# Fused quantised cross-attention product and low-rank feed-forward on one core: tile 7's second half of normalised x transposed by DMA instead of TensorE

## Chip, core and metric

One core of a Trainium2 chip runs the whole kernel. The metric is the device time of one execution in microseconds (us). Five engines have a part: TensorE (PE in the rows; its weight loads are PEld), VectorE (DVE), ScalarE (ACT), GpSimd (POOL) and SyncE (SP), whose queue issues most of the DMAs. ScalarE issues DMAs too; both queues are served by the core's 16 DMA engines.

## The reference

For x of shape 2 x 1024 x 2048 and a context of shape 2 x 2048 x 2048, with `fake_quant` rounding to 256 levels:

```
x = x + tanh(g_xattn) * (fake_quant(layernorm(x)) @ fake_quant(ctx))
x = x + tanh(g_ffn)   * (layernorm(x) @ (U * S @ V.T).T)
```

V and U are 2048 x 512, so the second step is done as two thin products.

## The kernel before

The 2048 rows of x are 16 tiles of 128 rows; tiles 0 to 7 belong to the first context matrix, tiles 8 to 15 to the second. A tile t goes through these steps:

- `load_x`: four DMAs of 128 x 512 into a ring of four tiles (`ring`); each waits until the tile four before has been stored. `quantise` and `op2` on ScalarE round the normalised tile to fp16 (`qn`), `q_transpose` (a DMA transpose on SyncE's queue) turns it over into `qT`.
- `s1`: the first product, tile by quantised context (`q2`), in four column units of 16 matmuls. VectorE (`x1_unit`) adds each unit to x.
- second layernorm; ScalarE (`x_hi_half`) and VectorE (`x_lo_half`) write the result as a high and a low fp16 part into `xs`, in two halves g = 0 and 1 of 1024 columns each. Each half is then transposed into `xT[:, g]`.
- `mm3`: V product of the transposed halves, 24 matmuls for g = 0 and then 24 for g = 1. ScalarE (`hid_hi`) and VectorE (`hid_lo`) write the result as two fp16 parts, `h_transpose` (a DMA transpose) turns them over.
- `mm4`: U product, four units of 12 matmuls in three PSUM banks in turn. VectorE (`y_unit`) adds each to x, `store` writes it out. Unit i may start once `y_unit` i-3 is done.

Two normalised halves are transposed by a DMA each (`x_transpose_half`, 128 x 2048 fp16, 512 KB) for all tiles but one: tile 7 (`X_PE`). For it TensorE does the transposes (`x_pieces(g)`, 16 pieces of 128 x 128 for each half, into two PSUM banks), and VectorE copies the two banks to `xT` (`xT_copy(g)`).

All engines run an order written out by hand. Around tile 7 TensorE's is `mm3(6)`, `x_pieces(0)`, `mm4(5)`, `x_pieces(1)`, `mm3(7)`, `mm4(6)`, `colsum_of_sums(0)` to `(2)`, `mm4(7, 0, 3)` and then `s1_part(8, 0)`. In the same stretch the second context matrix is brought in: 32 chunks of 512 KB, loaded by DMAs that ScalarE issues (`refill`) right after the chunk that it has read (`op1`, line 925: to uint8, read from `stage`, `corr`, `qn` or `q2` itself), turned into fp16 by GpSimd (line 293), and summed by VectorE (`k_sum`) for the column corrections. ScalarE's own order there is chunks 17 to 21, `hid_hi(6)`, chunks 22 to 25, `sums1(8)`, chunks 26 to 29, `quantise(8)`, `op2(8)`, chunks 30 and 31, `hid_hi(7)`. SyncE's queue is in order, and it waits at the head: four stores of tile 4, four loads of tile 8, `h_transpose(6)`, then `turn(5, False)`, which is stores of tile 5 in turn with loads of tile 9, then `q_transpose(8)`, `h_transpose(7)`.

Of the kernel before, what the change touches and what calls it, by code (L numbers as in the profile page):

```python
# [7 lines left out]
def gated_block_program(nc, x, ctx_in, params, U_t, S, V, out):  # L8
    f32, bf16, f16 = mybir.dt.float32, mybir.dt.bfloat16, mybir.dt.float16
# [3 lines left out]
    P = 128  # L13
# [7 lines left out]
    TB = SEQ // P  # L21
# [8 lines left out]
    X_PE = TB - 1  # L30
# [14 lines left out]
    with es:  # L45
# [14 lines left out]
        xs = sb("xs", [P, 2, 2, HW], f16)  # L60
        xT = sb("xT", [P, 2, 2, KT // 2, P], f16)
# [145 lines left out]
        unit_bank = lambda t, n: bank[4 * (n % 2) + t] if t < G else bank[(s_unit(t, n) - NQ * G) % 3]  # L207
        colsum_bank = lambda b, n: bank[4 * (n % 2) + 3] if b == 0 else bank[(0, 1, 3, 4)[n]]
        h_bank = lambda u: bank[3 + u % 2]
        x_dma = lambda u: u + 1 - (u > X_PE)  # L210
        x_bank = lambda g, half: bank[(2 * g + half) % 3]
        y_bank = lambda i: bank[5 + i % 3]
        k_sums = lambda n: xn[:, 0:W].bitcast(f16) if n == 0 else xs[:, n // 3, (n - 1) % 2, :]
        chunk = lambda c: (c // CB, c % CB // CQ, c % CQ)
# [129 lines left out]
        def _(sp):  # L344
            def load_x(t, n):
                if t >= R:
                    sp.wait_ge(y_stored[t % R][n], 16 * (t // R))
                sp.dma_start(xq(t, n), x_rows[t * P:(t + 1) * P, n * W:(n + 1) * W]).then_inc(x_in[t % R][n], 16)
# [51 lines left out]
            def h_transpose(u):  # L400
                sp.wait_ge(h_hi, u + 1)
                sp.wait_ge(h_lo, u + 1)
                if u == 0:
                    sp.wait_ge(sq_done, 16)
                if u == NT - 1:
                    sp.wait_ge(p_done, 2 * NP * len(PAIRS))
                elif u == TB - 1:
                    sp.wait_ge(ctx_u8, act_u8(STAGE1_CHUNK))
                elif u == 5:
                    sp.wait_ge(s1_done, S1_END(6))  # L410
                elif u >= 1:
                    sp.wait_ge(y_done, NQ * {6: 5, 8: 7}.get(u, u))
                sp.dma_start_transpose(hT_of(u), hs.rearrange("p k w -> p (k w)")).then_inc(hT_in, 16)
# [175 lines left out]
        def _(pe):  # L589
# [27 lines left out]
            def colsum_of_sums(n):  # L617
                pe.wait_ge(k_summed, KS * (n + 1))
                if n < 2:
                    pe.wait_ge(xT_copied, 4)  # L620
                else:
                    pe.wait_ge(h_hi, TB - 1 + n - 2)
                    pe.wait_ge(h_lo, TB - 1 + n - 2)
                for a in range(CK):
                    mm = nc.tensor.matmul(colsum_bank(1, n)[:, :], ones_h[:, :], k_sums(n)[:, a * W:(a + 1) * W],
                                          start=(a == 0), stop=(a == CK - 1))
                mm.then_inc(colsum_done, 1)
# [113 lines left out]
            def mm3(u):  # L741
                if u == 0:
                    pe.wait_ge(corr_ready, NQ - 1)
                elif u == 1:
                    pe.wait_ge(x1_ready, unit(0, NQ - 1) + 1)
                    pe.wait_ge(norm_ready, 1)
                else:
                    pe.wait_ge(h_hi, u - 1)
                    pe.wait_ge(h_lo, u - 1)
                if u == TB:  # L750
                    pe.wait_ge(corr_ready, 2 * NQ)
                for g in range(2):
                    if u == X_PE:
                        pe.wait_ge(xT_copied, 2 * g + 2)
                    else:
                        pe.wait_ge(xT_in[g], 16 * x_dma(u))
                    for a, k in enumerate(KORD[g]):
                        if u == 0 and a % 2 == 0:
                            pe.wait_ge(split_hi, VORD.index(k // 2) + 1)
                        for half in range(2):  # L760
                            nc.tensor.matmul(h_bank(u)[:, :], x_home(u, g)[:, half, k % 8, :], v_hl[:, k, 0, :],  # L761
                                             start=(g == 0 and a == 0 and half == 0), stop=False)
                    for a, k in enumerate(KORD[g]):
                        if u == 0 and a % 2 == 0:
                            pe.wait_ge(split_lo, VORD.index(k // 2) + 1)
                        mm = nc.tensor.matmul(h_bank(u)[:, :], x_home(u, g)[:, 0, k % 8, :], v_hl[:, k, 1, :],  # L766
                                              start=False, stop=(g == 1 and a == 7))
                    mm.then_inc(mm3_half, 1)

            def x_pieces(g):  # L770
                pe.wait_ge(xs_hi, 2 * X_PE + g + 1)
                pe.wait_ge(xs_lo, 2 * X_PE + g + 1)
                for half in range(2):
                    if 2 * g + half < 3:
                        pe.wait_ge(x1_ready, S1_END(TB - 1) - (2, 1, 0)[2 * g + half])
                    else:
                        pe.wait_ge(xT_copied, 1)
                    dst = x_bank(g, half)[:, :].bitcast(f16)
                    for k in range(8):
                        mm = nc.tensor.transpose(dst[:, k * P:(k + 1) * P], xs[:, g, half, k * P:(k + 1) * P], ident[:, :])  # L780
                    mm.then_inc(xT_written, 1)

            def mm4(u, n0=0, n1=NQ):
# [133 lines left out]
        def _(act):  # L917
# [85 lines left out]
            def x_hi_half(u, g):  # L1003
                scale, bias = ln2[:, u % 2, 8:9], ln2[:, u % 2, 9:10]
                act.wait_ge(ln2_ready, u + 1)
                if u in first_of and g == 0:
                    act.wait_ge(p_done, 2 * NP * (first_of[u] + 1))
                if u - 1 == X_PE:
                    act.wait_ge(xT_written, 2 * g + 2)
                elif u > 0:  # L1010
                    act.wait_ge(xT_in[g], 16 * x_dma(u - 1))
                nc.scalar.activation(xs[:, g, 0, :], xhalf(u, g), ACT.Identity, bias=bias, scale=scale).then_inc(xs_hi, 1)  # L1012
                if u in XN_ACT:
                    act.wait_ge(xs_lo, 2 * u + g)
                    nc.scalar.activation(xn[:, :], xhalf(u, g), ACT.Identity, bias=bias, scale=scale).then_inc(xn_ready, 1)  # L1015
# [226 lines left out]
        def _(dve):  # L1242
# [125 lines left out]

            def early_t1():
                for g in range(2):  # L1370
                    dve.wait_ge(xT_in[g], 16 * x_dma(EARLY[0] - 1))
                for c in range(2):
                    b11, b12 = [k_piece(flat2(b_part(n, 0)), c, 2 * HW) for n in (2, 3)]
                    tt(k_piece(e_t1, c, 2 * HW), b12, b11, ALU.subtract).then_inc(e_t1_made, 1)
# [64 lines left out]
            def t4(q, c0, c1):  # L1439
                p, j = divmod(q, 2)  # L1440
                for c in range(c0, c1):
                    if c == 0:
                        dve.wait_ge(t_made, 4 * j + 4)
                        if j == 0:
                            for g in range(2):
                                dve.wait_ge(xT_in[g], 16 * x_dma(PAIRS[p][0] - 1))
                        else:
                            dve.wait_ge(p_done, pdone(q - 1, P4))
                    tt(k_piece(t4_room, c, HW), k_piece(flat2(b_part(2 * j, 1)), c, HW),
                       k_piece(t2_room[j], c, HW), ALU.subtract).then_inc(t4_made, 1)  # L1450
# [67 lines left out]
                x_lo_half(u, 0)  # L1518
                x_lo_half(u, 1)

            def xT_copy(g):
                for half in range(2):
                    dve.wait_ge(xT_written, 2 * g + half + 1)
                    dve.wait_ge(mm3_half, 2 * (X_PE - 1) + g + 1)
                    nc.vector.tensor_copy(xT[:, g, half, :, :].rearrange("p k w -> p (k w)"),
                                          x_bank(g, half)[:, :].bitcast(f16)).then_inc(xT_copied, 1)
# [7 lines left out]
            def k_sum(n, i):  # L1534
                c = CB + CQ * n + i
                dve.wait_ge(q2_pool, pool_count(c))
                if i == 1 and n == 0:
                    dve.wait_ge(xs_lo, 2 * TB)
                elif i == 1:
                    dve.wait_ge(xT_written, 2 + 2 * (n // 3))  # L1540
                else:
                    dve.wait_ge(k_summed, KS * n + i - 1)
                tt(k_sums(n), q2_chunk(c - 1) if i == 1 else k_sums(n), q2_chunk(c), ALU.add).then_inc(k_summed, 1)
# [358 lines left out]
```

## Time and profile before

| | us |
|---|---|
| median of 3 runs | 586.42 |
| lowest, highest | 584.85, 586.98 |
| profiled execution, device time | 585.22 |
| its span in the trace | 583.4 |
| TensorE busy in it | 566.6 (97%) |

Times in the rows are us from the start of the span, and "[... <-X]" is idle time of the engine just before and what ended it. Matmuls are pipelined: the times from one matmul's start to the next one's tell what it costs, not its length. `x3` in a row is a run of three instructions. For a DMA, the length of a queue row (SPq, ACTq) is the time of issuing; the time to landing is told by other rows.

### The profile page before, as it was taken

The numbers are of one execution on the slowest core, as the hardware profiler recorded it, in microseconds if no ns is written. First come the engines' busy times: TensorE is split into PE (matmuls) and PEld (weight loads), VectorE is DVE, ScalarE is ACT, GpSimd is POOL, SyncE is SP. The second block draws the span as 40 slices with busy tenths as digits, with TensorE's granted clock in tenths as the row PEclk, the third lists the DMA queues.
The fourth block names the chain that finished last, engine by engine and source line by source line (L and its number), as shares of the span: only waits on it lengthen the run. The fifth ranks groups of instructions, "written<-read, shape, count | busy, mean of one in ns | idle before, by whom it ended". The sixth has DMA issues, their size and how long they took to land.

```text
span 583.4 us, 7494 instructions
## 1 busy us (share of the span) xinstructions
PE 566.6 (97%) x2672; PEld 258.1 (44%) x2672; DVE 450.0 (77%) x795; ACT 251.7 (43%) x282; POOL 195.8 (34%) x146
## 2 busy tenths in 40 slices
PE   1999999999999999999999999999999999999997
PEld 0444444444444444444444444444444444444444
DVE  6878889997978851788879798788598986889222
ACT  5899978823214525537883612103530135003200
POOL 2999750000750038836543720210044005310000
PEclk9999999999999999999999999999999999999999
DMA  8999995639558986799986362424854086403612
GB/s 277 387 387 386 345 265 135 127 107 188 138 157 170 256 175 164 278 222 386 272 202 174 61 137 52 126 73 80 216 102 143 2 184 159 126 1 74 161 55 108
DMA packets 146997, 103.00 MB, mean 177 GB/s; under 512 B 109840, under 2 KB 110096, under 8 KB 146960
## 3 DMA queue, kind: packets, MB, share of 16 engines
q1 hardware_dynamic: 137968, 85.22, 55.5%
q10 hardware_dynamic: 8992, 17.30, 9.3%
q8 instruction: 21, 0.34, 0.2%
q14 instruction: 16, 0.13, 0.1%
HBM read 58.99 MB, written 16.78 MB: 130 GB/s over the span
## 4 chain that ended last, share of the span: by engine, by line
PE 82%; DVE 5%; DMA 5%; ACT 4%; issue 2%; SPq 1%; POOL 1%; ACTq 1%; DVEq 0%
PE bank L761 17%; PE bank L653 15%; PE bank L698 12%; PE bank L811 8%; PE bank L812 8%; PE bank L766 8%; PE bank L816 8%; DMA stage<-in_ctx_dram 3%; PE bank L612 2%; PE bank L728 2%; ACT u8r L925 2%; DMA ring<-in_x_dram 1%; DVE qn L1314 1%; POOL q L293 1%; DVE xn L1512 1%
## 5 line engine op out<-in xcount | busy, mean ns | idle before, releaser
L299 POOL TENSOR_SCALAR ring<-ring,bvec 128x2048 f32<-128x2048 f32 x16 | 34.5, 2155 | 256.6 <-DVE bvec L1326 256.6
L653 PE MATMUL bank<-q,qT 128*128 128x512 f16 x448 | 104.3, 383 | 0.7 <-DMA qT<-qn 0.7
L761 PE MATMUL bank<-v_hl,xT 128*128 128x512 f16 x448 | 101.3, 379 | 0.0
L304 POOL TENSOR_TENSOR ring<-ring,corr 128x512 f32<-128x512 f32 x64 | 87.6, 1399 | 19.1 <-ACT corr L1040 18.1
L293 POOL TENSOR_SCALAR q<-u8r,const 128x1024 f16<-128x1024 uint8 x52 | 67.0, 1298 | 36.8 <-ACT u8r L925 33.4
L811 PE MATMUL bank<-u_hl,hbuf 128*128 128x512 f16 x208 | 78.9, 379 | 0.1
L812 PE MATMUL bank<-u_hl,hbuf 128*128 128x512 f16 x208 | 78.9, 379 | 0.0
L996 ACT ACTIVATE ln<-ln,const 128x1 f32<-128x1 f32 x16 | 4.7, 293 | 151.7 <-DVE ln L1485 151.2
L653 PEld LDWEIGHTS bank<-q,qT 128*128 128x128 f16 x448 | 44.0, 98 | 54.8 <-issue 1.4
L761 PEld LDWEIGHTS bank<-v_hl,xT 128*128 128x128 f16 x448 | 43.8, 98 | 52.4 <-DMA xT<-xs 0.2
L1559 DVE SCALAR_TENSOR_TENSOR ring<-bank,cy,ring 128x512 f32<-128x512 f32 x63 | 45.9, 743 | 13.5 <-PE bank L816 13.4
L816 PE MATMUL bank<-u_hl,hbuf 128*128 128x512 f16 x208 | 53.4, 379 | 0.0
L766 PE MATMUL bank<-v_hl,xT 128*128 128x512 f16 x224 | 52.9, 379 | 0.0
L1515 DVE TENSOR_TENSOR xs<-xn,xs 128x1024 f16<-128x1024 f32 x32 | 42.9, 1340 | 12.7 <-ACT xn L1015 6.4
L1012 ACT ACTIVATE xs<-ring,ln 128x1024 f16<-128x1024 f32 x32 | 38.6, 1234 | 16.8 <-DVE ln L1497 10.6
L1283 DVE BATCH_NORM_STATS2 st<-ring 128x6 f32<-128x512 f32 x56 | 35.2, 679 | 8.4 <-DMA ring<-in_x_dram 8.3
L1475 DVE SCALAR_TENSOR_TENSOR ring<-bank,const,ring 128x512 f32<-128x512 f32 x42 | 31.3, 746 | 9.8 <-PE bank L698 9.8
L1531 DVE SCALAR_TENSOR_TENSOR hbuf<-bank,hbuf 128x512 f16<-128x512 f32 x16 | 11.0, 687 | 33.5 <-ACT hbuf L1027 33.4
L766 PEld LDWEIGHTS bank<-v_hl,xT 128*128 128x128 f16 x224 | 21.9, 98 | 26.5
L925 ACT ACTIVATE u8r<-stage,par,const 128x1024 uint8<-128x1024 f32 x22 | 27.2, 1236 | 13.9 <-DMA stage<-in_ctx_dram 9.8
L1344 DVE SCALAR_TENSOR_TENSOR ring<-bank,const,ring 128x512 f32<-128x512 f32 x36 | 26.7, 741 | 8.4 <-PE bank L653 5.0
L612 PE MATMUL bank<-q,ones_h 128*128 128x512 f16 x64 | 20.4, 402 | 11.9 <-POOL q L293 11.9
(200 smaller groups left out, 832.7 us busy)
## 6 DMA issues: line engine op xcount, KB each, us to landing
out_dram<-ring SPq DMA_DIRECT2D x63, 256.0 KB, 3.5
ring<-in_x_dram SPq DMA_DIRECT2D x62, 256.0 KB, 4.3
v_hl<-in_ctx_dram SPq DMA_DIRECT2D x26, 512.0 KB, 11.5
stage<-in_ctx_dram ACTq DMA_DIRECT2D x17, 512.0 KB, 6.0
u_hl<-in_L_ffn_V_dram SPq DMA_DIRECT2D x8, 512.0 KB, 11.5
corr<-in_ctx_dram ACTq DMA_DIRECT2D x8, 512.0 KB, 6.8
stage<-in_ctx_dram SPq DMA_DIRECT2D x6, 512.0 KB, 11.4
q<-in_ctx_dram ACTq DMA_DIRECT2D x4, 512.0 KB, 10.7
```

The lines of the kernel that those rows point to most:

```text
L293: nc.gpsimd.tensor_scalar(q2_chunk(c), u8r[:, c % NU8, :], C_NC2, 1.0, ALU.add, ALU.mult)\
L304: nc.gpsimd.tensor_tensor(xq(t, n), xq(t, n), corr[:, n * W:(n + 1) * W], ALU.add).then_inc(x1_pre, 1)
L653: mm = nc.tensor.matmul(unit_bank(t, n)[:, :], qT_of(t)[:, k, :], q2[:, n, k, :], start=(k == 0), stop=(k == KT - 1))
L698: mm = nc.tensor.matmul(pbank(q, k)[:, :], left[:, i, :], right[:, i, :], start=(i == 0 and k in (P1, P2, P5)), stop=(i == KH - 1), skip_g ...
L761: nc.tensor.matmul(h_bank(u)[:, :], x_home(u, g)[:, half, k % 8, :], v_hl[:, k, 0, :], start=(g == 0 and a == 0 and half == 0), stop=False)
L766: mm = nc.tensor.matmul(h_bank(u)[:, :], x_home(u, g)[:, 0, k % 8, :], v_hl[:, k, 1, :], start=False, stop=(g == 1 and a == 7))
L811: nc.tensor.matmul(y_bank(i)[:, :], t_hi[:, r, :], u_hl[:, n, r, 0, :], start=(r == 0), stop=False)
L812: nc.tensor.matmul(y_bank(i)[:, :], t_lo[:, r, :], u_hl[:, n, r, 0, :], start=False, stop=False)
L816: mm = nc.tensor.matmul(y_bank(i)[:, :], t_hi[:, r, :], u_hl[:, n, r, 1, :], start=False, stop=(r == RT - 1))
L925: nc.scalar.activation(u8r[:, c % NU8, :], flat2(SPOT[c][0]), ACT.Identity, bias=P_Z2, scale=C_R2).then_inc(ctx_u8, 1)
L1515: tt(xs[:, g, 1, :], xn[:, :], xs[:, g, 0, :], ALU.subtract).then_inc(xs_lo, 1)
L1559: stt(xq(u, n), y_bank(i)[:, :], cy[:, n:n + 1], xq(u, n), ALU.mult, ALU.add).then_inc(y_ready, 1)
```

## The change

Tile 7's half g = 0 stays on TensorE and VectorE. Half g = 1 is transposed by a DMA on SyncE's queue, put between the loads of tile 8 and `h_transpose(6)`. `x_pieces(1)` leaves TensorE's order and `xT_copy(1)` VectorE's. The second half of `mm3(7)`, the later users of `xs` half 1 (`x_hi_half(8, 1)`, `k_sum` of the fourth column group) wait for the DMA's semaphore `xT_in[1]` instead. The DMA waits for the high and low parts of tile 7's half 1 and for the end of `mm3(6)`, which reads the same half of `xT`.

```
                 load_x(8, n)
+            x_transpose_half(7, 1)
             h_transpose(6)
...
-                    if u == X_PE:
-                        pe.wait_ge(xT_copied, 2 * g + 2)
+                    if u == X_PE and g == 0:
+                        pe.wait_ge(xT_copied, 2)
                     else:
-                        pe.wait_ge(xT_in[g], 16 * x_dma(u))
+                        pe.wait_ge(xT_in[g], 16 * x_dma(u, g))
...
-            x_pieces(0)
+            x_pieces()
             mm4(5)
-            x_pieces(1)
             mm3(7)
...
-                if u - 1 == X_PE:
-                    act.wait_ge(xT_written, 2 * g + 2)
+                if u - 1 == X_PE and g == 0:
+                    act.wait_ge(xT_written, 2)
...
+                elif i == 1 and n < 3:
+                    dve.wait_ge(xT_written, 2)
                 elif i == 1:
-                    dve.wait_ge(xT_written, 2 + 2 * (n // 3))
+                    dve.wait_ge(xT_in[1], 16 * x_dma(X_PE, 1))
...
-            xT_copy(0)
+            xT_copy()
...
             y_unit(5, 3)
-            xT_copy(1)
             quantise(8)
```

TensorE from the end of `mm4(5)` to the end of `mm3(7)`, before (L780 is `x_pieces`, L761 and L766 are `mm3`):

```order
L816 MATMUL bank<-u_hl,qT 128x512 x4
L780 MATMUL bank<-ident,xs 128x128 [waits x1_ready,xs_lo,xs_hi]
L780 MATMUL bank<-ident,xs 128x128 x7
L780 MATMUL bank<-ident,xs 128x128 [waits xT_copied]
L780 MATMUL bank<-ident,xs 128x128 x7
L761 MATMUL bank<-v_hl,xT 128x512 [waits xT_copied,h_lo,h_hi]
L761 MATMUL bank<-v_hl,xT 128x512 x15
L766 MATMUL bank<-v_hl,xT 128x512 x8
L761 MATMUL bank<-v_hl,xT 128x512 [waits xT_copied]
L761 MATMUL bank<-v_hl,xT 128x512 x15
L766 MATMUL bank<-v_hl,xT 128x512 x8
```

and after (the same lines are L814, L762 and L767 there):

```order
L814 MATMUL bank<-u_hl,qT 128x512 x4
L762 MATMUL bank<-v_hl,xT 128x512 [waits xT_copied,h_lo,h_hi]
L762 MATMUL bank<-v_hl,xT 128x512 x15
L767 MATMUL bank<-v_hl,xT 128x512 x8
L762 MATMUL bank<-v_hl,xT 128x512 [waits xT_in1]
L762 MATMUL bank<-v_hl,xT 128x512 x15
L767 MATMUL bank<-v_hl,xT 128x512 x8
```

The 16 pieces are gone, and the second half of `mm3(7)` waits for the DMA's semaphore.

SyncE's queue at the same place, before and after in one (L424 are stores, L348 loads of x, L413 `h_transpose`, L393 `x_transpose_half`):

```order
 L424 DMA out_dram<-ring 128x512 x4
 L348 DMA ring<-in_x_dram 128x512 x4
+L393 DMA_TRANSPOSE xT<-xs 128x16x128
 L413 DMA_TRANSPOSE hbuf<-hbuf 128x8x128
 L424 DMA out_dram<-ring 128x512 x2
```

One DMA is added, and `h_transpose(6)` and all that follows stand behind it.

## Rows read from the trace of the kernel before

**Rows 1.** Page: busy time by engine.

```profile
PE 566.6 (97%) x2672; PEld 258.1 (44%) x2672; DVE 450.0 (77%) x795; ACT 251.7 (43%) x282; POOL 195.8 (34%) x146
```

**Rows 2.** TensorE's timeline, 267 to 303 us: start, length, line, tiles, count.

```profile
267.09 1.89 PE L766 MATMUL bank<-v_hl,xT 128*128 128x512 f16 x8
...
280.07 1.06 PE L780 MATMUL bank<-ident,xs 128*128 128x128 f16 x16
280.96 3.62 PE L761 MATMUL bank<-v_hl,xT 128*128 128x512 f16 x16
...
286.14 3.62 PE L761 MATMUL bank<-v_hl,xT 128*128 128x512 f16 x16
...
291.32 0.38 PE L811 MATMUL bank<-u_hl,hbuf 128*128 128x512 f16 x1
...
299.10 0.38 PE L811 MATMUL bank<-u_hl,hbuf 128*128 128x512 f16 x1
...
302.98 0.38 PE L811 MATMUL bank<-u_hl,stage 128*128 128x512 f16 x1
```

**Rows 3.** VectorE's timeline, 280 to 299 us.

```profile
280.98 1.27 DVE L1525 COPY xT<-bank 128x1024 f16<-128x1024 f16 x2
284.01 0.15 DVE L1299 TENSOR_SCALAR ln<-ln 128x1 f32<-128x1 f32 x1 [1.76 <-ACT ln L987]
...
297.36 1.40 DVE L1559 SCALAR_TENSOR_TENSOR ring<-bank,cy,ring 128x512 f32<-128x512 f32 x2
```

**Rows 4.** VectorE and TensorE's weight loads at 255 us: `y_unit(4, 0)`, `mm4(4, 3)`.

```profile
255.06 0.74 DVE L1559 SCALAR_TENSOR_TENSOR ring<-bank,cy,ring 128x512 f32<-128x512 f32 x1
...
255.85 0.10 PEld L811 LDWEIGHTS bank<-u_hl,hbuf 128*128 128x128 f16 x1 [0.64 <-DVE ring L1559]
```

**Rows 5.** ScalarE's timeline, 277 to 297 us.

```profile
277.11 1.24 ACT L925 ACTIVATE u8r<-corr,par,const 128x1024 uint8<-128x1024 f32 x1
...
287.37 1.24 ACT L925 ACTIVATE u8r<-stage,par,const 128x1024 uint8<-128x1024 f32 x1 [0.51 <-ACT u8r L925]
...
294.89 1.23 ACT L925 ACTIVATE u8r<-stage,par,const 128x1024 uint8<-128x1024 f32 x1
296.02 0.57 ACT L1027 ACTIVATE hbuf<-bank 128x512 f16<-128x512 f32 x1
```

**Rows 6.** SyncE's queue, 246 to 275 us: start, time of issuing.

```profile
246.07 8.46 SPq L393 DMA_TRANSPOSE xT<-xs  x2
...
260.50 7.92 SPq L348 DMA_DIRECT2D ring<-in_x_dram  x4
274.05 1.23 SPq L413 DMA_TRANSPOSE hbuf<-hbuf  x1
```

**Rows 7.** Issued at 246.03, 247.78 and 246.07, 265.17, 270.42, 286.89: us to landing.

```profile
corr<-in_ctx_dram ACTq DMA_DIRECT2D x1, 512.0 KB, 4.2
...
corr<-in_ctx_dram ACTq DMA_DIRECT2D x1, 512.0 KB, 7.0
xT<-xs SPq DMA_TRANSPOSE x1, 8.9
...
corr<-in_ctx_dram ACTq DMA_DIRECT2D x1, 512.0 KB, 11.9
...
stage<-in_ctx_dram ACTq DMA_DIRECT2D x1, 512.0 KB, 11.1
...
stage<-in_ctx_dram ACTq DMA_DIRECT2D x1, 512.0 KB, 7.1
```

**Rows 8.** Transposes issued at 274.05 and 297.38 us: us to landing.

```profile
hbuf<-hbuf SPq DMA_TRANSPOSE x1, 7.9
...
stage<-hbuf SPq DMA_TRANSPOSE x1, 3.1
```

**Rows 9.** Stretches: us; busy PE, PEld, DVE, ACT, POOL; clock, DMA share, GB/s.

```profile
273.00:278.00 5.00, 5.00 (x25) 2.29 (x24) 4.79 (x7) 4.01 (x4) 4.42 (x4) 1.00 1.05 388
...
282.00:288.00 6.00, 6.00 (x29) 2.73 (x28) 3.92 (x10) 4.95 (x6) 2.66 (x2) 1.00 0.75 237
```

More of the change, by code:

```diff
@@ L209, in gated_block_program @@
         h_bank = lambda u: bank[3 + u % 2]
-        x_dma = lambda u: u + 1 - (u > X_PE)
-        x_bank = lambda g, half: bank[(2 * g + half) % 3]
+        x_dma = lambda u, g: u + 1 - (g == 0 and u > X_PE)
+        x_bank = lambda half: bank[half]
         y_bank = lambda i: bank[5 + i % 3]
@@ L619, in colsum_of_sums @@
                 if n < 2:
-                    pe.wait_ge(xT_copied, 4)
+                    pe.wait_ge(xT_copied, 2)
                 else:
@@ L752, in mm3 @@
                 for g in range(2):
-                    if u == X_PE:
-                        pe.wait_ge(xT_copied, 2 * g + 2)
+                    if u == X_PE and g == 0:
+                        pe.wait_ge(xT_copied, 2)
                     else:
-                        pe.wait_ge(xT_in[g], 16 * x_dma(u))
+                        pe.wait_ge(xT_in[g], 16 * x_dma(u, g))
                     for a, k in enumerate(KORD[g]):
@@ L768, in mm3, with x_pieces @@
                     mm.then_inc(mm3_half, 1)
-            def x_pieces(g):
-                pe.wait_ge(xs_hi, 2 * X_PE + g + 1)
-                pe.wait_ge(xs_lo, 2 * X_PE + g + 1)
+            def x_pieces():
+                pe.wait_ge(xs_hi, 2 * X_PE + 1)
+                pe.wait_ge(xs_lo, 2 * X_PE + 1)
                 for half in range(2):
[L774 to L778, printed above, removed]
+                    pe.wait_ge(x1_ready, S1_END(TB - 1) - (2, 1)[half])
+                    dst = x_bank(half)[:, :].bitcast(f16)
                     for k in range(8):
-                        mm = nc.tensor.transpose(dst[:, k * P:(k + 1) * P], xs[:, g, half, k * P:(k + 1) * P], ident[:, :])
+                        mm = nc.tensor.transpose(dst[:, k * P:(k + 1) * P], xs[:, 0, half, k * P:(k + 1) * P], ident[:, :])
                     mm.then_inc(xT_written, 1)
@@ L1007, in x_hi_half @@
                     act.wait_ge(p_done, 2 * NP * (first_of[u] + 1))
-                if u - 1 == X_PE:
-                    act.wait_ge(xT_written, 2 * g + 2)
+                if u - 1 == X_PE and g == 0:
+                    act.wait_ge(xT_written, 2)
                 elif u > 0:
-                    act.wait_ge(xT_in[g], 16 * x_dma(u - 1))
+                    act.wait_ge(xT_in[g], 16 * x_dma(u - 1, g))
                 nc.scalar.activation(xs[:, g, 0, :], xhalf(u, g), ACT.Identity, bias=bias, scale=scale).then_inc(xs_hi, 1)
@@ L1370, in early_t1 @@
                 for g in range(2):
-                    dve.wait_ge(xT_in[g], 16 * x_dma(EARLY[0] - 1))
+                    dve.wait_ge(xT_in[g], 16 * x_dma(EARLY[0] - 1, g))
                 for c in range(2):
@@ L1445, in t4 @@
                             for g in range(2):
-                                dve.wait_ge(xT_in[g], 16 * x_dma(PAIRS[p][0] - 1))
+                                dve.wait_ge(xT_in[g], 16 * x_dma(PAIRS[p][0] - 1, g))
                         else:
@@ L1519, in x_lo, with xT_copy @@
                 x_lo_half(u, 1)
-            def xT_copy(g):
+            def xT_copy():
                 for half in range(2):
[L1523 to L1526, printed above, removed]
+                    dve.wait_ge(xT_written, half + 1)
+                    dve.wait_ge(mm3_half, 2 * (X_PE - 1) + 1)
+                    nc.vector.tensor_copy(xT[:, 0, half, :, :].rearrange("p k w -> p (k w)"),
+                                          x_bank(half)[:, :].bitcast(f16)).then_inc(xT_copied, 1)
             def hid_lo(u):
```

## Prediction

> **What bounds the kernel now.** I read first the page: TensorE is busy for 97% of the span [rows 1], so a change counts only by what it takes off TensorE's row of work or by the idle time that it puts into it. Second, TensorE's timeline around tile 7: from 280 to 303 us each matmul follows the one ahead without a bracket, so nothing waits there now [rows 2]. Third, the timelines of VectorE and ScalarE, read backwards from the matmuls that they release, for the distance that each release has to the matmul behind it: that is the room in which the other engines may get late, and it shrinks by whatever TensorE gains. Fourth, the DMAs one by one, from issue to landing, since the change puts 512 KB of transpose into a stretch in which the DMA engines have no free time: 388 GB/s at a share of 1.05 [rows 9].
>
> **The pieces.** TensorE starts the 16 pieces at 280.07 and the first matmul of mm3(7) at 280.96 [rows 2]. Without them mm3(7) starts at 280.07: 0.89 us less, all of it on the path. Nothing else leaves TensorE.
>
> **The two copies.** They take 1.27 us of VectorE, and right behind them VectorE idles 1.76 us for ScalarE's root [rows 3]. Without them it idles 1.27 us longer. Cost and gain 0; the cover is ScalarE's row of chunks, which ends at the same time as before.
>
> **The wait in mm3(7).** The DMA can't be issued before mm3(6) has ended, at 267.09 + 1.89 = 268.98 [rows 2]; SyncE's queue has issued tile 8's last load by 260.50 + 7.92 = 268.42 [rows 6], so it goes out at about 269.0. The second half of mm3(7) wants it at 286.14 - 0.89 = 285.25 [rows 2]. Early bound of its landing: the half issued at 246.07 took 8.9 us [rows 7], which gives 277.9. Late bound: it is served when the whole backlog is through, which is when the context chunk issued at 270.42 lands, 281.5, plus its own share of the DMA engines. That share I take from two chunks: 4.2 us for the one issued just ahead of the transpose of 246.07, and 7.0 us for the one issued behind it, so 2.8 us [rows 7]. That gives 284.3. Both bounds lie ahead of 285.25: the wait costs 0. Queued behind it on TensorE is everything, so if it were late, each us would be one of the total.
>
> **The queue behind the new DMA.** h_transpose(6) goes out at 274.05 when VectorE has made its input [rows 6]. Two transposes of this size took 8.46 us to issue, 4.2 each [rows 6]: SyncE would be free at 273.2, just ahead. Landing was 7.9 us later, at 282.0 [rows 8]; with 2.8 us more, 284.8, against a need at 291.32 - 0.89 = 290.43 [rows 2]. Cost 0. The stores of tile 5, the loads of tile 9, q_transpose(8) and h_transpose(7) stand behind it too; the last of these is a rival below.
>
> **The loads beside it.** Here the sum is decided. In the same 10 us ScalarE reads context chunks as they land: the one issued at 265.17 took 11.9 us, landed at 277.07 and was read from 277.11 on [rows 5, 7]. ScalarE then has work without a gap worth naming through to hid_hi(7) at 296.02 [rows 5], hid_lo(7) on VectorE waits for that, and the y_unit right behind it, (6, 0), starts at 297.36 [rows 3]. So if this chunk lands d us later, hid_hi(7) and y_unit(6, 0) come d us later. mm4(6, 3) needs y_unit(6, 0) (unit i behind y_unit i-3). One such unit lasts 0.74 us and its matmul can load 0.05 us behind its end [rows 4]: it is released at 297.36 + 0.74 + 0.05 = 298.15, and starts now at 299.10 [rows 2]. With the gain it would start at 298.21. The room is 0.95 us now and 0.06 us then: **the gain of 0.89 us fits just in, and every us of d beyond 0.06 is a us of TensorE idle**. The change in time is the larger of -0.89 and d - 0.95.
>
> What is d? The trace of before has no transpose in such a backlog except one, and I bound it from both sides. *Low end, 0:* h_transpose(6) was issued at 274.05 with four chunks ahead of it and took 7.9 us, where the same transpose in a calmer place (297.38) took 3.1 [rows 8]; the chunk issued just ahead of the transpose of 246.07 landed in 4.2 us, unharmed, while the one behind it took 7.0 [rows 7]. Both say that a transpose takes its turn behind the chunks issued ahead of it, and that only those issued behind it pay. The chunk of 265.17 was issued 3.8 us ahead of the new DMA: d = 0. *High end, 4.2:* the new transpose is served at once and takes its 2.8 us, and h_transpose(6), half as large, comes right behind it and takes 1.4 more before the chunk has landed. The nearest row in time, load and kind is that of 274.05, so I take d = 0. The chunk that pays then is that of 270.42: it landed at 281.5 and is read at 287.37 [rows 5, 7], 5.8 us of room for 2.8.
>
> The page "DMA: Bandwidth & Descriptors" of the Trainium skill, section "Queues, rings and completion order", speaks against this choice: each DMA engine goes round between the queues that have work, a packet at a time, so a transpose on SyncE's queue would start beside ScalarE's chunks and not behind them. By that rule the chunk of 265.17 is late and the first rival holds; by the row of 274.05 it isn't.
>
> **Sum.** 585.22 (profiled execution) - 0.89 + 0 + 0 + 0 = 584.3 us. The median of the runs stands 1.2 us above that execution, so the forecast for the median is 586.42 - 0.89 = 585.5 us. VectorE and ScalarE follow TensorE in the later tiles, so I expect the 0.89 us to reach the end.
>
> **Rivals.**
> 1. *The transpose shares the DMA engines with the chunks (slower).* d = 2.8: mm4(6, 3) waits, 2.8 - 0.95 = +1.85, 588.3 us; with h_transpose(6) in front of the chunk as well, d = 4.2, +3.25, 589.7 us. It decides from d = 0.95 on. For it: the 7.0 us of the chunk behind a transpose, and DMA engines with no free time. Against it: the 7.9 and the 4.2 us. The skill's rule above is this case.
> 2. *The same 2.8 us turn up later.* The chunk issued at 286.89 took 7.1 us, landed at 293.99 and was read at 294.89 [rows 5, 7]: 0.90 us of room. If the added work is still in the queues then, d = 2.8 - 0.9 = 1.9 and the change is +0.95, 587.4 us. Against it: from 282 to 288 us the DMA engines moved 237 GB/s only [rows 9], so there is room to catch up.
> 3. *SyncE's queue is held.* If issuing stalls until the backlog is through, all behind it goes out late, h_transpose(7) too. It landed at 297.38 + 3.1 = 300.5 [rows 8], and is wanted at 302.98 - 0.89 = 302.1 [rows 2]: 1.6 us of room. Late by 2.5 us, it would eat the gain: 586.4 us.
> 4. *The change doesn't do what it says:* the wait on the DMA takes the place of the pieces. At the worst it starts when the backlog is through, 281.5, and then takes the 7.0 us of a DMA in mixed traffic [rows 7]: 288.5, 3.2 us of idle time in mm3(7), +2.3, 588.8 us.
>
> **How the numbers follow.** Forecast (no new wait above 0.3 us) 0.50; rival 1 0.25, of which 0.06 at its high end; rival 2 0.10; rival 3 0.10; rival 4 0.05. About 0.5% is what a measurement of this kernel can tell from no change, 2.9 us: below 583.5 or above 589.3. Even the whole gain is a third of that, so faster has only the scatter of the runs, 0.02; slower is the high end of rival 1 and some scatter, 0.08; same 0.90. The range runs from 584.7 (the forecast less 0.8 of scatter; the three runs spread over 2.1) to 588.5 (rival 1's first price): outside are the high end of rival 1 and tails.
>
> **What would show each step.** Right: mm3(7) starts 0.89 us earlier with no bracket, its second half too; the chunk of 265.17 is still read at 277.1 and hid_hi(7) starts at 296.0; the new transpose takes over 9 us to land, and the chunk of 270.42 lands near 284. Wrong by rival 1: ScalarE waits for a DMA at 277 us, hid_hi(7) starts at 298 or later, and the weight load of mm4(6, 3) has a bracket ending in VectorE's y_unit. By rival 2 that bracket with the wait at 294; by rival 3 a bracket at mm4(7, 0) that ends in a DMA; by rival 4 one in the middle of mm3(7). What would make the forecast wrong beyond these: a place behind 310 us where TensorE has under 0.89 us of room, which gives the gain back unseen.

## Result

| | us |
|---|---|
| kernel before, median of 14 runs | 585.22 (584.58 to 587.51) |
| changed kernel, median of 14 runs | 586.31 (585.04 to 588.27) |
| ratio, changed to before | 1.0020, 95% interval 1.0011 to 1.0029 |

The change costs 1.1 us, 0.2%. That lies within the stated range, but on the other side of zero from the forecast of -0.9. The changed kernel's runs fall into groups: five of them lie from 585.0 to 585.4 and six from 587.0 to 588.3, where the kernel before has two (587.0 and 587.5). An execution at a lower granted clock is left out of the ratios below (one each in e9 and e10).

### The profile after

Its span is 583.4 us, as before, but it had reached the stretch in question 0.45 us earlier for reasons that lie ahead of the change. So times are compared from a common mark, the start of the first 16 pieces: 268.82 us before, 268.37 after. TensorE's timeline after (start, length, line, tiles; L778 are the pieces, L762 mm3, L809 the first matmul of a unit of mm4), which answers to [rows 2]:

```profile
268.37 1.06 PE L778 MATMUL bank<-ident,xs 128*128 128x128 f16 x16
...
279.63 3.62 PE L762 MATMUL bank<-v_hl,xT 128*128 128x512 f16 x16
...
284.81 3.62 PE L762 MATMUL bank<-v_hl,xT 128*128 128x512 f16 x16
...
299.02 0.39 PE L809 MATMUL bank<-u_hl,hbuf 128*128 128x512 f16 x1 [1.10 <-DVE ring L1558]
...
302.91 0.38 PE L809 MATMUL bank<-u_hl,stage 128*128 128x512 f16 x1
...
341.33 3.62 PE L762 MATMUL bank<-v_hl,xT 128*128 128x512 f16 x16
```

From the mark to mm3(7) it is 11.26 us, and was 12.14: the gain of the pieces is there (0.88 us), and the second half of mm3(7) starts without a bracket. Then mm4(6, 3) waits for VectorE. At mm3(8), 341.33, TensorE is 72.96 us from the mark, and was 341.40 - 268.82 = 72.58: a loss of 0.38 us in this execution, -0.89 + 1.27.

VectorE and ScalarE after, which answer to [rows 3] and [rows 5] (L1558 is y_unit, L922 reads a context chunk, L1024 is hid_hi):

```profile
298.22 1.40 DVE L1558 SCALAR_TENSOR_TENSOR ring<-bank,cy,ring 128x512 f32<-128x512 f32 x2
```

```profile
275.89 1.24 ACT L922 ACTIVATE u8r<-q,par,const 128x1024 uint8<-128x1024 f32 x1 [1.36 <-DMA q<-in_ctx_dram]
277.42 1.24 ACT L922 ACTIVATE u8r<-corr,par,const 128x1024 uint8<-128x1024 f32 x1 [0.28 <-DMA corr<-in_ctx_dram]
...
289.36 1.24 ACT L922 ACTIVATE u8r<-corr,par,const 128x1024 uint8<-128x1024 f32 x1 [0.44 <-DMA corr<-in_ctx_dram]
...
296.88 0.57 ACT L1024 ACTIVATE hbuf<-bank 128x512 f16<-128x512 f32 x1
```

hid_hi(7) stands 28.51 us behind the mark, and stood 27.20: d = 1.31. The first 0.76 of it is there at the chunk read at 277.42. The rest comes with the chunk read at 289.36, for which ScalarE waits now and didn't before.

SyncE's queue after, which answers to [rows 6]:

```profile
268.62 8.30 SPq L393 DMA_TRANSPOSE xT<-xs  x1
277.04 3.71 SPq L413 DMA_TRANSPOSE hbuf<-hbuf  x1
...
296.42 3.00 SPq L375 DMA_TRANSPOSE qT<-qn  x1
299.53 1.24 SPq L413 DMA_TRANSPOSE stage<-hbuf  x1
```

The new transpose needs 8.3 us to be issued. h_transpose(6) goes out 3 us later than before. Behind it stand the stores of tile 5, which take 9.3 us to land where the first two took 6.4 and 5.6, and the loads of tile 9, which wait for these stores; so q_transpose(8) and h_transpose(7) are late too, the latter by 2.2 us. The landings, issued at 264.83, 268.62, 277.04 and 278.69, each row by itself from a list of DMAs:

```profile
corr<-in_ctx_dram ACTq DMA_DIRECT2D x1, 512.0 KB, 12.6
...
xT<-xs SPq DMA_TRANSPOSE x1, 15.5
...
hbuf<-hbuf SPq DMA_TRANSPOSE x1, 12.5
...
corr<-in_ctx_dram ACTq DMA_DIRECT2D x1, 512.0 KB, 10.6
```

The transpose lands at 284.1, against a need at 284.8; h_transpose(6) at 289.5, against 290.0. The last row is the chunk that is read at 289.36; the same chunk took 5.8 us in the kernel before. And the stretches, against [rows 9] (us; busy PE, PEld, DVE, ACT, POOL; clock, DMA share, GB/s):

```profile
273.00:278.00 5.00, 5.00 (x25) 2.28 (x24) 4.79 (x7) 3.36 (x4) 3.95 (x3) 1.00 1.06 294
...
282.00:288.00 6.00, 6.00 (x29) 2.74 (x28) 3.36 (x9) 4.95 (x6) 2.35 (x2) 1.00 1.18 166
```

From 273 to 278 us the DMA engines move 294 GB/s where they moved 388. Finer stretches show where that comes from:

```profile
273.50:274.50 1.00, 1.00 (x7) 0.44 (x5) 0.90 (x3) 1.00 (x1) 1.00 (x1) 1.00 0.36 20
...
275.00:278.00 3.00, 3.00 (x16) 1.37 (x14) 2.90 (x4) 1.82 (x2) 2.44 (x3) 1.00 1.09 390
```

For about 1.2 us they move next to nothing (20 GB/s), and then the old rate again with the transpose's packets among the chunks'. Such a stall stands in all eight traces with a transposing DMA at this place of the queue (after, e2, e3, e5, e6, e8, e9, e10; 25 GB/s from 274 to 275 in e2, 11 from 273.75 to 274.75 in e9), and from 273 to 278 us in none of the five others (e4, with a plain DMA there, has 393 GB/s). What stalls them isn't known.

From 282 to 288 us they move only 166 GB/s at a share of 1.18, where before there were 237 at 0.75. From 282 to 286 a packet of ScalarE's queue takes 0.28 us, and took 0.09 (116 packets in 50.6% of 16 engines' time, and 259 in 36.5%). This is when the chunk issued at 278.69 is under way.

### The profile page after: what moved, and what is told of

Read it like the earlier page. It is cut to its first block, busy times and chain, and to the rows that moved or that the text cites. A ratio compares the mean times of both kernels' runs of the same rounds, so it can differ in the third digit from the quotient of the medians.

```text
span 583.4 us, 7459 instructions
## 1 busy us (share of the span) xinstructions
PE 565.9 (97%) x2656; PEld 257.7 (44%) x2656; DVE 448.5 (77%) x793; ACT 252.0 (43%) x282; POOL 194.7 (33%) x146
## 4 chain that ended last, share of the span: by engine, by line
PE 74%; DMA 9%; ACT 6%; DVE 5%; issue 3%; SPq 1%; ACTq 1%; POOL 1%; DVEq 0%
PE bank L654 15%; PE bank L762 14%; PE bank L699 12%; PE bank L809 7%; PE bank L814 7%; PE bank L767 7%; PE bank L810 7%; DMA corr<-in_ctx_dram 4%; DMA stage<-in_ctx_dram 3%; ACT u8r L922 3%; PE bank L613 2%; PE bank L729 2%; DMA ring<-in_x_dram 2%; ACTq L929 1%; DVE qn L1311 1%
## 5 line engine op out<-in xcount | busy, mean ns | idle before, releaser
L762 PE MATMUL bank<-v_hl,xT 128*128 128x512 f16 x448 | 101.3, 379 | 0.0
L809 PE MATMUL bank<-u_hl,hbuf 128*128 128x512 f16 x208 | 78.9, 379 | 1.2 <-DVE ring L1558 1.1
L293 POOL TENSOR_SCALAR q<-u8r,const 128x1024 f16<-128x1024 uint8 x52 | 65.5, 1267 | 39.2 <-ACT u8r L922 36.3
L762 PEld LDWEIGHTS bank<-v_hl,xT 128*128 128x128 f16 x448 | 43.9, 98 | 52.6
L1558 DVE SCALAR_TENSOR_TENSOR ring<-bank,cy,ring 128x512 f32<-128x512 f32 x63 | 45.9, 744 | 13.3 <-PE bank L814 13.2
L814 PE MATMUL bank<-u_hl,hbuf 128*128 128x512 f16 x208 | 53.4, 379 | 0.0
L767 PE MATMUL bank<-v_hl,xT 128*128 128x512 f16 x224 | 52.9, 379 | 0.0
L1009 ACT ACTIVATE xs<-ring,ln 128x1024 f16<-128x1024 f32 x32 | 38.6, 1234 | 16.5 <-DVE ln L1494 10.6
L1472 DVE SCALAR_TENSOR_TENSOR ring<-bank,const,ring 128x512 f32<-128x512 f32 x42 | 31.3, 746 | 9.8 <-PE bank L699 9.8
L767 PEld LDWEIGHTS bank<-v_hl,xT 128*128 128x128 f16 x224 | 21.9, 98 | 26.4
L922 ACT ACTIVATE u8r<-stage,par,const 128x1024 uint8<-128x1024 f32 x22 | 27.2, 1236 | 13.4 <-DMA stage<-in_ctx_dram 9.8
L809 PEld LDWEIGHTS bank<-u_hl,hbuf 128*128 128x128 f16 x208 | 20.4, 98 | 27.5 <-DVE ring L1558 3.6
```

Of the source, the lines that this page charges most:

```text
L293: nc.gpsimd.tensor_scalar(q2_chunk(c), u8r[:, c % NU8, :], C_NC2, 1.0, ALU.add, ALU.mult)\
L809: nc.tensor.matmul(y_bank(i)[:, :], t_hi[:, r, :], u_hl[:, n, r, 0, :], start=(r == 0), stop=False)
L814: mm = nc.tensor.matmul(y_bank(i)[:, :], t_hi[:, r, :], u_hl[:, n, r, 1, :], start=False, stop=(r == RT - 1))
L922: nc.scalar.activation(u8r[:, c % NU8, :], flat2(SPOT[c][0]), ACT.Identity, bias=P_Z2, scale=C_R2).then_inc(ctx_u8, 1)
L1558: stt(xq(u, n), y_bank(i)[:, :], cy[:, n:n + 1], xq(u, n), ALU.mult, ALU.add).then_inc(y_ready, 1)
```

## Experiments

The theory after the result had two parts. **A**: the transpose makes ScalarE's chunks late, so that y_unit(6, 0) is late for mm4(6, 3). **C**: it holds SyncE's queue, so that h_transpose(6) and (7) come late for mm4(6) and mm4(7). The rivals: **B**, mm3(7) waits for the new DMA itself in the slower executions; and that the pieces never give anything back. **D** and **E** ask whether the form of the DMA or its bytes do the harm.

In all tables "in the trace" is the way from the mark (the first pieces) to the start of mm3(8), less the 72.58 us of the kernel before. It is one execution; the ratio is from the timed runs, against the kernel before on the same chip.

### e1: the gain alone

```
-            x_transpose_half(7, 1)
```

(and `x_dma` counts one DMA less for half 1)

> As the changed kernel, but the new DMA isn't issued: the second half of mm3(7) reads what xT held for tile 6, so that half of tile 7's transpose is left out. It prices the pieces alone. Both theories: mm3(7) starts 0.89 us earlier and nothing waits behind it: -0.9 us against the kernel before. If it comes out at 0 or above, the loss of the changed kernel isn't from the DMA at all, and there is a place behind 310 us that gives the gain back.

Measured: ratio 0.9986 (0.9974 to 0.9997), -0.8 us; in the trace 71.68, -0.90. The first matmul of mm4(7) is where it should be, with no bracket since the mark:

```profile
269.16 1.06 PE L777 MATMUL bank<-ident,xs 128*128 128x128 f16 x16
...
302.43 0.38 PE L808 MATMUL bank<-u_hl,stage 128*128 128x512 f16 x1
```

The price of the pieces and its way to the end were right. The whole loss against this kernel, about 1.9 us, comes from the DMA.

### e2: the DMA alone

```
+            sp.dma_start_transpose(qT[:, 0, :, :], flat2(xs[:, 1, :, :])).then_inc(extra_in, 16)
             h_transpose(6)
```

(into the kernel before, with its pieces; later writers of `qT` half 0 and of `xs` half 1 wait for `extra_in`)

> The kernel before with all its pieces and copies, plus one more DMA transpose of the same 512 KB at the same place of SyncE's queue, into a free buffer (half of qT) that no matmul reads. It prices the DMA alone. Theory A (the transpose makes ScalarE's context chunks late, hid_hi(7) and y_unit(6, 0) come late, mm4(6, 3) waits): the same end as the changed kernel, +0.4 to +1.1 us, with a bracket at mm4(6, 3). Theory B (mm3(7) waits for the new DMA in the slower executions, which landed 0.5 us ahead of its need in the profile): nothing reads it here, so at most +0.4.

Measured: ratio 1.0007 (0.9997 to 1.0017), +0.4 us; in the trace 72.78, +0.20. The chunk lateness is there (hid_hi(7) 27.96 us from the mark, d = 0.76), inside the room of 0.95, and mm4(6, 3) doesn't wait. The weight load of mm4(7) does, and for the other reason:

```profile
269.19 8.19 SPq L536 DMA_TRANSPOSE qT<-xs  x1
```

```profile
303.28 0.10 PEld L818 LDWEIGHTS bank<-u_hl,stage 128*128 128x128 f16 x1 [0.52 <-DMA stage<-hbuf]
```

So in this trace the DMA costs something where no one reads its result (the interval of the runs reaches below 1), and it does so by SyncE's queue. From the mark h_transpose(6) goes out 3.3 us later and the first stores of tile 5 4.6 us later; these take 8.9 us to land where they took 6.4, and h_transpose(7) is 2.7 us late behind the loads that wait for them. The hold of 8.2 us and the slower stores aren't separated here. The expectation's bracket at mm4(6, 3) was missed, and the two theories' numbers met at +0.4, so this run doesn't rule out B; the two traces of the changed kernel don't show it (e5).

### e3: y_unit(6, 0) ahead of hid_lo(7)

```
+            y_unit(6, 0)
             hid_lo(7)
             row_correction(8)
-            y_unit(6, 0)
```

> The changed kernel with one move on VectorE: y_unit(6, 0) ahead of hid_lo(7), so that mm4(6, 3) no longer stands behind ScalarE's chunks. Theory A: the wait of 1.1 us at mm4(6, 3) goes, the next need is mm4(7, 0) with some 0.4 us of room, so -0.9 to -0.3 us against the kernel before. Theory B (late landing in mm3(7)) or C (SyncE's queue held, h_transpose(7) late): it stays at +0.5 to +1.1.

Measured: ratio 1.0003 (0.9990 to 1.0016), +0.2 us; in the trace 73.64, +1.06. The wait at mm4(6, 3) is gone as meant, and others have its place:

```profile
302.93 0.60 PE L626 MATMUL bank<-xs,ones_h 128*128 128x512 f16 x2 [0.64 <-DVE xs L1542]
304.38 0.39 PE L809 MATMUL bank<-u_hl,stage 128*128 128x512 f16 x1 [0.84 <-DMA stage<-hbuf]
```

The first is the column sums, whose sum on VectorE (L1542) stands behind hid_lo(7); the second is h_transpose(7), issued at 300.40 behind q_transpose(8) at 297.22. A third is smaller: the weight load of mm4(6, 0) waits 0.45 us for h_transpose(6). Both parts, A and C, are at work here, so the removal of one wait uncovers others. The forecast of A alone, -0.9 to -0.3, was missed.

### e4: a plain DMA of the same bytes

```
-            x_transpose_half(7, 1)
+            sp.dma_start(xT[:, 1, :, :, :]..., xs[:, 1, :, :]...).then_inc(xT_in[1], 16)
```

(with the same waits ahead of it)

> The changed kernel with a plain DMA of the same 512 KB from xs to xT in place of the transposing one: tile 7's second half isn't transposed. Theory D (it is the form, a transpose of very many small packets that hangs behind the chunks and holds SyncE's queue 8 us): the plain DMA issues in under 1 us, lands within 8 us, the chunks are late by at most 1 us; 0 to -0.9 us. Theory E (it is the bytes, any 512 KB in a full stretch): d of 1 to 1.5 us as in the changed kernel, +0.3 to +1.1.

Measured: ratio 0.9994 (0.9982 to 1.0005), -0.35 us; in the trace 72.46, -0.12.

```profile
269.22 0.55 SPq L534 DMA_DIRECT2D xT<-xs  x1
```

```profile
xT<-xs SPq DMA_DIRECT2D x1, 512.0 KB, 8.0
```

```profile
277.84 1.24 ACT L925 ACTIVATE u8r<-corr,par,const 128x1024 uint8<-128x1024 f32 x1 [0.69 <-DMA corr<-in_ctx_dram]
...
298.89 0.39 PE L812 MATMUL bank<-u_hl,hbuf 128*128 128x512 f16 x1 [0.37 <-DVE ring L1561]
```

The weight load of mm4(7, 0) waits too, 0.54 us, for h_transpose(7), which takes 4.8 us to land here (3.1 before).

Neither D nor E alone. The bytes make the first chunks late in either form (0.58 us from the mark at the chunk of 277.84, against 0.76). The transposing form adds the hold of the queue, 8.3 us against 0.55, and the landing of 15.5 against 8.0.

### e5: the changed kernel once more

> The changed kernel itself, on the chip of the runs beside it, for a second trace. Theory A (ScalarE's chunks late) and theory C (SyncE's queue held for 8 us, so that h_transpose(6), tile 9's loads, q_transpose(8) and h_transpose(7) come late) both say +0.5 to +1.2 us; A has its bracket at mm4(6, 3), C has one at mm4(6, 0) or mm4(7, 0) that ends in a DMA.

Measured: ratio 1.0013 (1.0001 to 1.0026), +0.8 us. The trace is of the slowest of the 12 executions (588.92), 74.31 from the mark, +1.73:

```profile
293.35 0.39 PE L809 MATMUL bank<-u_hl,hbuf 128*128 128x512 f16 x1 [0.80 <-DMA hbuf<-hbuf]
...
302.67 0.39 PE L809 MATMUL bank<-u_hl,hbuf 128*128 128x512 f16 x1 [1.38 <-DVE ring L1558]
```

```profile
293.00 1.24 ACT L922 ACTIVATE u8r<-corr,par,const 128x1024 uint8<-128x1024 f32 x1 [1.30 <-DMA corr<-in_ctx_dram]
```

```profile
hbuf<-hbuf SPq DMA_TRANSPOSE x1, 13.1
```

Both brackets that A and C named stand in one trace: mm4(6, 0) waits for h_transpose(6), issued at 280.17 and 13.1 us on its way, and mm4(6, 3) for y_unit(6, 0) behind a chunk that ScalarE waited 1.3 us for. Without the first wait the second would be longer by as much: y_unit(6, 0) stands behind ScalarE's chain until 301.87, long after its unit of mm4(6) is ready. So h_transpose(6) costs nothing by itself here. mm3(7) has no bracket, so B isn't seen in either trace of the changed kernel; nor in e3 and e8, where the same DMA lands 1.3 and 1.6 us ahead of its need. It landed 0.7 and 0.6 us ahead in the two of the changed kernel.

### e6: a shorter queue of chunks

```
-                act.dma_start(SPOT[c][0], ctx_k[...])
+                part = slice(0, 1) if SPOT[c][1] in room_in else slice(0, CK)
+                act.dma_start(SPOT[c][0][:, part, :], ctx_k[...][:, part, :])
```

> The changed kernel with the four context chunks that go to q2 itself loaded by half (256 KB each; the other half of those chunks is left out), so that the queue of ScalarE's loads is 1 MB shorter when the new transpose is issued. If the loss is contention (theories A and C alike), SyncE's queue is held well under 8 us, the transpose lands before 282, no wait is left and the gain shows: -0.9 to -0.4 us. If the hold of SyncE's queue comes from the transpose itself, whatever else is in flight, it stays at +0.5 to +1.1.

Measured: ratio 0.9983 (0.9975 to 0.9992), -1.0 us; in the trace 71.69, -0.89: the whole gain.

```profile
268.53 6.79 SPq L393 DMA_TRANSPOSE xT<-xs  x1
```

```profile
xT<-xs SPq DMA_TRANSPOSE x1, 11.0
```

The hold is still 6.8 us, more than expected ("well under 8"), and does no harm: the transpose lands at 279.5, ScalarE's chunks have no bracket, and h_transpose(7) is issued at 295.96. With 1 MB less in the queue the change does what it is for: the loss needs the full queue. The stall of the DMA engines is in this trace too (77 GB/s from 273.5 to 274.25), but ScalarE's chunks land ahead of their reads, so nothing waits for it. This run shortens the chunks' own way too, so it doesn't part A from C.

### e7: the new DMA behind h_transpose(6)

```
-            x_transpose_half(7, 1)
             h_transpose(6)
+            x_transpose_half(7, 1)
```

> The changed kernel with the new DMA behind h_transpose(6) on SyncE's queue instead of ahead of it. Theory A: the chunk that was issued at 265.17 isn't touched, d falls to about 0 there; the transpose is issued at 275 and lands at about 285, so mm3(7)'s second half waits 0 to 1.5 us: -0.9 to +0.6. Theory C: the hold of the queue only begins 6 us later and ends later, tile 9's loads and h_transpose(7) come as late as before or later: +0.5 to +2.

Measured: ratio 1.0093 (1.0080 to 1.0107), +5.4 us; in the trace +5.74. Further out than either expectation:

```profile
290.14 5.31 PE L762 MATMUL bank<-v_hl,xT 128*128 128x512 f16 x16 [4.78 <-DMA xT<-xs]
```

```profile
xT<-xs SPq DMA_TRANSPOSE x1, 14.3
```

The DMA is issued at 275.81 and takes 14.3 us again, so mm3(7) waits 4.8 us. The 16 matmuls behind the wait take 5.31 us where they took 3.62: TensorE's granted clock was 1.00 through the wait and until 290.5, 0.50 (the lower of its levels of 1.2 and 2.4 GHz) from 291 to 294, and 1.00 again from 294.5. That is 1.7 us of the 5.7. Theory A was right in its first half: the chunk read at 277 us isn't late (ScalarE is back at its place before, sums1(8) 10.27 us from the mark against 10.47). But the transpose then makes the chunk issued at 278.13 late, as in the changed kernel: it takes 11.8 us, and ScalarE waits 1.55 us for it.

### e8: h_transpose(7) ahead of q_transpose(8)

```
-            q_transpose(8)
             h_transpose(7)
+            q_transpose(8)
```

(on top of e3)

> The changed kernel with y_unit(6, 0) ahead of hid_lo(7) on VectorE (as the third experiment) and, on SyncE's queue, h_transpose(7) ahead of q_transpose(8). If what was left in the third experiment is h_transpose(7) behind a late q_transpose(8) (theory C), mm4(7, 0) has over 1 us of room again: -0.7 us against the kernel before, with a wait of about 0.4 us left at mm4(6, 0) in some executions. If theory A alone were true, this does no more than the third one: +0.2.

Measured: ratio 1.0031 (1.0020 to 1.0041), +1.8 us; in the trace +1.42. The wait at mm4(7, 0) is gone, as expected, but the gain isn't there:

```profile
303.82 1.91 ACT L978 ACTIVATE qn<-ring 128x2048 uint8<-128x2048 f32 x1 [7.42 <-DMA qT<-qn]
```

```profile
310.67 7.07 PE L654 MATMUL bank<-q,qT 128*128 128x512 f16 x32 [1.03 <-ACT corr L1037]
```

h_transpose(7) has to wait for hid_lo(7), so q_transpose(8) behind it goes out at 298.53. ScalarE's sums1(9) waits for q_transpose(8), the column corrections come behind it, and s1(8) waits for those. sums1(9) starts 5.0 us later from the mark than in the kernel before, and s1(8) 1.2 us later than the gain of the pieces would have it: this third chain had 3.8 us of room, and the swap of two transposes used up more than that.

### e9 and e10: half the DMA

```
-            x_transpose_half(7, 1)
+            sp.dma_start_transpose(xT[:, 1, 0, :, :], xs[:, 1, 0, :]).then_inc(xT_in[1], 16)
             h_transpose(6)
...
             mm4(5)
+            x_low_piece()
...
             y_unit(5, 3)
+            xT_low_copy()
```

(waits left out; 8 pieces and one copy come back for the low parts; e10 has e3's move too)

> The changed kernel with the DMA cut to half its size: only the high parts of tile 7's second half go by DMA (256 KB, same place of the queue), the low parts by 8 pieces on TensorE and one copy on VectorE as before. Theory C (a transpose of 512 KB behind a full queue holds SyncE 8 us because its packets don't fit; one of 256 KB was issued in 1.2 us at the same place): no hold, h_transpose(6) issued by 274.1, no wait at mm4(6, 0) or mm4(7, 0). The pieces give 0.45 us, the chunk is late by about half of 0.7 us, inside the room: -0.45 us. If the hold is there all the same: 0 to +0.8.

> The same as e9 with y_unit(6, 0) ahead of hid_lo(7) on VectorE: -0.45 us too if nothing waits in e9, and a little under e9 if mm4(6, 3) still waits there.

Measured: e9 0.9994 (0.9985 to 1.0004), in the trace 72.13, -0.45; e10 0.9986 (0.9977 to 0.9995), in the trace 72.15, -0.43. Neither has a bracket on the matmuls from the mark to s1(8).

```profile
268.55 1.24 SPq L533 DMA_TRANSPOSE xT<-xs  x1
272.96 3.97 SPq L413 DMA_TRANSPOSE hbuf<-hbuf  x1
```

```profile
xT<-xs SPq DMA_TRANSPOSE x1, 12.8
```

Issued in 1.24 us, so SyncE reaches h_transpose(6) in time; that one takes 3.97 us to issue in turn, but SyncE is free at 276.9, and not at 280.8 as in the changed kernel. The landing is still 12.8 us (13.5 in e10), against 15.5 for twice the size. In the medians e9 stands at -0.6 and e10 at -0.8 us. ScalarE's lateness differs between the two traces: hid_hi(7) is 27.40 us from the mark in e9 and 28.19 in e10, d = 0.20 and 0.99. With the gain of 0.45 the room at mm4(6, 3) is 0.95 - 0.45 = 0.50, so by an estimate e9's order would have cost some 0.5 us in an execution like that of e10's trace, and there e3's move is what saves it.

### e11: the control

```
+            y_unit(6, 0)
             hid_lo(7)
```

(the same move as e3, in the kernel before)

> The kernel before with that one move on VectorE alone: mm4(6, 3) had 0.95 us of room already, so 0. It is the control for the third experiment: if it gains by itself, part of what the third one gained over the changed kernel isn't about the DMA.

Measured: ratio 0.9993 (0.9984 to 1.0002), and 0.00 in the trace. It can't be told from no change; nor can it from the -0.4 us that its median shows, so how much of e10's 0.8 us is the move's alone stays open. **e10 is below both kernels with its interval**, by 0.14% of the kernel before; its trace shows 0.43 us of that.

### All of them

| | ratio (95%) | in the trace, us | bracket on TensorE, (w) on a weight load alone |
|---|---|---|---|
| changed | 1.0020 (1.0011 to 1.0029) | +0.38 | mm4(6, 3) |
| e1 no DMA | 0.9986 (0.9974 to 0.9997) | -0.90 | none |
| e2 DMA added to before | 1.0007 (0.9997 to 1.0017) | +0.20 | mm4(7, 0) (w) |
| e3 y_unit first | 1.0003 (0.9990 to 1.0016) | +1.06 | mm4(6, 0) (w), column sums, mm4(7, 0) |
| e4 plain DMA | 0.9994 (0.9982 to 1.0005) | -0.12 | mm4(6, 3), mm4(7, 0) (w) |
| e5 changed again | 1.0013 (1.0001 to 1.0026) | +1.73 | mm4(6, 0), mm4(6, 3), mm4(7, 0) (w) |
| e6 1 MB less in flight | 0.9983 (0.9975 to 0.9992) | -0.89 | none |
| e7 behind h_transpose(6) | 1.0093 (1.0080 to 1.0107) | +5.74 | mm3(7) |
| e8 h_transpose(7) first | 1.0031 (1.0020 to 1.0041) | +1.42 | s1(8), column sums |
| e9 half the DMA | 0.9994 (0.9985 to 1.0004) | -0.45 | none |
| e10 half, y_unit first | 0.9986 (0.9977 to 0.9995) | -0.43 | column sums (w) |
| e11 y_unit first in before | 0.9993 (0.9984 to 1.0002) | 0.00 | none |

## The prediction, step by step

**The pieces: right.** 0.89 us forecast, 0.88 in the trace, 0.8 in e1's runs, and it reaches the end.

**The copies: right.** VectorE idles 3.46 us where it idled 1.76: 1.27 for the copies, and the rest since ScalarE's root comes later. Nothing waits for it.

**The wait in mm3(7): right, with some luck.** The late bound, 284.3 for 285.25, is nearly what happened (284.1 for 284.8). It is so since two errors nearly cancel: counted from the mark, the last chunk of the backlog landed 0.9 us later than in the kernel before, and the transpose 2.2 us behind it and not 2.8. Nor did the transpose wait for its turn behind the backlog; its packets ran among the chunks'. Of the 0.95 us of room that the bound leaves, 0.68 was there.

**The queue behind: wrong.** I took 4.2 us to issue from the pair at 246.07, which met a much shorter queue of chunks. It was 8.3, and h_transpose(6) landed at 289.5 where I had 284.8. I had the mechanism as rival 3 at 0.10, priced it by h_transpose(7) alone, and didn't see h_transpose(6). In the changed kernel's second trace mm4(6, 0) waits 0.8 us for it, inside the longer wait of the chunks. Of the three DMAs that TensorE waits for, h_transpose(7) had the least room in the first trace: it lands at 302.64 for 302.91, h_transpose(6) at 289.50 for 289.99, and the new one at 284.13 for 284.81.

**The loads beside: the step that decided, and it failed.** The relation was right: with d = 1.31, d - 0.95 gives +0.36, and the trace has +0.38. In the second trace hid_hi(7) is 29.77 us from the mark, d = 2.57, which gives +1.62 for +1.73. What failed is the size, d = 0. The choice of the low end was half right: the chunk issued ahead of the transpose was late by 0.76 us only, not by 2.8. But I checked the room of the chunk issued just behind the transpose (270.42) and passed over the next one, issued at 278.4. The prediction doesn't name it. By then the transpose and the held h_transpose(6) were the backlog. It took 10.6 us where it had taken 5.8, and used up its 4.3 us of room and 0.44 more. That is rival 2's mechanism, with a chunk 8 us earlier than the one that I named, and rival 1 at a quarter of its price on top.

The row that I took d = 0 from was misread as well. At 274.05 there were five chunks on their way, not four, and h_transpose(6) didn't wait for them. In the kernel before, SyncE's queue (q1) moved nothing from 275 to 278 us, and from 278 to 279, with three chunks still to land (278.5, 280.0, 281.5), its packets ran beside those of ScalarE's (q10; packets, MB, share of 16 engines):

```profile
q10 hardware_dynamic: 149, 0.29, 80.3%
q1 hardware_dynamic: 243, 0.06, 29.2%
```

So of the 7.9 us the first 4 went by before it moved anything, for a reason that stays open, and the rest beside the chunks. That it landed late says nothing on whether chunks ahead of it go unharmed.

d isn't one number either. Over the five traces with this DMA of 512 KB at this place it is 0.19 (e8), 0.76 (e2), 1.31, 1.62 (e3) and 2.57 (e5), while hid_hi(7) without a DMA there lies 26.47 to 27.20 us from the mark (e11, e1, before). The lateness is clear of that scatter in all but e8, where it is just above, and it varies by more than the whole room.

**The skill's rule.** The section "Queues, rings and completion order" of "DMA: Bandwidth & Descriptors" in the Trainium skill, which I had set against the forecast, has the engines go round between queues by the packet. The trace agrees. In the changed kernel, from 275 to 278 us:

```profile
q10 hardware_dynamic: 536, 1.03, 89.0%
q1 hardware_dynamic: 531, 0.14, 19.9%
```

One packet for one, but ScalarE's are of 1.9 KB and the transpose's of about 0.26 KB. So the transpose got an eighth of the bytes, which fits its late landing, and a chunk ahead of it that was late by 0.76 us, not by the 2.8 that rival 1 had put on the rule.

**How the numbers followed.** The time 585.5 came nearer (0.8 us off) than the change (2.0 us off) by luck: the median of three runs that it starts from, 586.42, stood 1.2 us above that of 14. Two cases of 0.10 and one of 0.25 weren't separate: one cause, a transpose in a full queue, fed them all at once, and each pulled the same way. With room of 0.06 us at the tightest place, 0.50 for "no wait above 0.3" was too much.

Open: the traces explain +0.4 and +1.7 us of two executions, and the median of +1.1 lies between. Which waits the other slow executions had isn't known; mm3(7) with 0.6 to 0.7 us of room may be one. No run parts the lateness of the chunks from the hold of SyncE's queue.

## To carry to other kernels

When work leaves the bounding engine, the room of every wait behind it shrinks by the same amount, so list all releases in the stretch (here hid_hi, three transposes, the column sums, sums1) with their room less the gain, and ask of the new DMA whether it delays several at once. A DMA transpose put into a full stretch cost three ways here that its own landing doesn't show: it held the queue that issues it, it made the loads ahead of it late by 0.2 to 1.1 us, and a load issued 10 us behind it paid most (10.6 us for 5.8). A wait that lies ahead of a longer one of another chain costs nothing by itself, so a bracket isn't yet a price. If it must be there, cut it until it is issued without a hold, and move only the part of the work that fits into the room.

## What the runs showed of the hardware

- A transposing DMA of 512 KB with six loads of 512 KB and three or four of 256 KB still to land took 8.0 to 9.0 us to issue and 14.6 to 15.5 to land (after, e2, e3, e5, e8); with 1 MB less ahead 6.8 and 11.0 (e6). A plain DMA of the same bytes at the same place took 0.55 and 8.0 (e4). A transposing one of 256 KB took 1.24 us to issue and 12.8 and 13.5 to land (e9, e10), so landing hardly follows size there.
- Beside the loads the DMA engines took one packet of the transpose for one of the loads (531 and 536 from 275 to 278 us), of about 0.26 and 1.9 KB, and moved 390 GB/s.
- Shortly after the first such packets the DMA engines moved next to nothing for about 1 us, in all eight traces with a transposing DMA there (20 GB/s from 273.5 to 274.5 in the changed kernel). In the kernel before, with a transpose issued at 274.05, SyncE's queue moved nothing from 275 to 278.
- After 4.8 us of idle time TensorE's granted clock stayed at 1.00 for some 0.5 us of matmuls, then was 0.50 from 291 to 294 us and 1.00 from 294.5 (e7); the 1.1 us in the changed kernel left it at 1.00.
